# Router logits of a two-pass fp32 macaron block: rows moved past the split router instead of the router past the rows

## What is computed

```python
def route(x, router_w, bias):                    # x: rows x 128, router_w: 16 x 128
    logits = x @ router_w.T                      # one number per row and expert, in fp32
    s = sigmoid(logits) + bias
    # best 2 of 4 groups of experts, then the best 4 experts in them; weights normalised, times 2.5
    ...
h = silu(x @ gate_w[e]) * (x @ up_w[e])          # for each of 16 routed experts
y = sum_e weight[row, e] * (h @ down_w[e])       # plus 2 shared experts, unweighted
```

## Time and profile before

| | |
|---|---|
| median of three runs | 659.91 us |
| span of the profiled execution | 657.5 us |
| busy, PE (TensorE) | 648.0 us (99%) |
| busy, DVE (VectorE) | 550.5 us (84%) |
| busy, POOL (GpSimd) | 464.4 us (71%) |
| busy, ACT (ScalarE) | 400.7 us (61%) |
| granted TensorE clock | 1.000 in every stage |

### The profile page before, as it was taken

One profiled execution on the slowest core, in us unless ns is written; L12 is line 12 of the kernel. 1 busy time (PEld: TensorE's weight loads), 2 busy tenths in 40 slices (PEclk: granted clock), 3 DMA queues, 4 the chain that ended last, 5 costly groups with the idle time before them and its releaser, 6 DMA issues.

```text
span 657.5 us, 10122 instructions
## 1 busy us (share of the span) xinstructions
PE 648.0 (99%) x3043; PEld 534.3 (81%) x3043; DVE 550.5 (84%) x1468; ACT 400.7 (61%) x790; POOL 464.4 (71%) x400
## 2 busy tenths in 40 slices
PE   8999999999999999999999999999999999999997
PEld 7888888888788887888878888878878888888886
DVE  6899889797988979879798798896987979878674
ACT  5876666566675555755657556575564655655554
POOL 6997776767866678566785667766667677767664
PEclk9999999999999999999999999999999999999999
DMA  9827352816236152271532804526147172543510
GB/s 232 271 63 262 93 227 50 273 32 212 83 85 235 32 192 99 59 264 32 158 134 49 273 17 122 201 48 247 50 86 248 44 226 93 161 157 83 221 32 33
DMA packets 107542, 90.07 MB, mean 137 GB/s; under 512 B 67408, under 2 KB 89824, under 8 KB 107488
## 3 DMA queue, kind: packets, MB, share of 16 engines
q1 hardware_dynamic: 107488, 89.43, 43.1%
HBM read 79.45 MB, written 9.96 MB: 136 GB/s over the span
## 4 chain that ended last, share of the span: by engine, by line
PE 91%; DVE 7%; DMA 1%; issue 0%; SPq 0%; ACT 0%; DVEq 0%
PE gateP L512 10%; PE upP L512 9%; PE gateP L516 9%; PE gateP L513 9%; PE yP L516 9%; PE yP L512 9%; PE upP L516 9%; PE yP L513 9%; PE upP L513 9%; PE prepP L548 1%; DVE T L1226 1%; PE attP L565 1%; DVE ast L1153 1%; DVE A L1257 1%; DVE parts L961 1%; PE attP L617 1%
## 5 line engine op out<-in xcount | busy, mean ns | idle before, releaser
L396 POOL TENSOR_TENSOR A_lo<-A,A_hi 128x512 fp32r<-128x512 f32 x287 | 370.7, 1294 | 175.2 <-ACT A_hi L869 174.6
L895 ACT ACTIVATE gateP<-gateP 128x512 f32<-128x512 f32 x252 | 146.5, 581 | 161.9 <-PE gateP L516 161.1
L1226 DVE TENSOR_TENSOR T<-gateP,CB 128x512 f32<-128x512 f32 x252 | 172.8, 686 | 65.6 <-ACT gateP L895 63.3
L869 ACT CAST A_hi<-A 128x512 fp32r<-128x512 f32 x287 | 176.5, 615 | 51.0 <-DVE A L1257 48.8
L1257 DVE TENSOR_TENSOR A<-upP,T 128x512 f32<-128x512 f32 x254 | 175.7, 692 | 8.7
L512 PE MATMUL gateP<-XT_hi,W_hi 128*128 128x512 f32 x288 | 117.9, 409 | 2.9 <-DVE T L1226 2.8
L512 PE MATMUL yP<-A_hi,W_hi 128*128 128x512 f32 x288 | 113.0, 392 | 0.0
L516 PE MATMUL gateP<-XT_lo,W_hi 128*128 128x512 f32 x288 | 112.5, 391 | 0.0
L516 PE MATMUL yP<-A_lo,W_hi 128*128 128x512 f32 x288 | 112.4, 390 | 0.0
L513 PE MATMUL gateP<-XT_hi,W_lo 128*128 128x512 f32 x288 | 112.4, 390 | 0.0
L513 PE MATMUL yP<-A_hi,W_lo 128*128 128x512 f32 x288 | 112.1, 389 | 0.0
(11 more groups left out here) (229 smaller groups left out, 652.3 us busy)
## 6 DMA issues: line engine op xcount, KB each, us to landing
CB<-combT SPq DMA_DIRECT2D x126, 512.0 KB, 6.7
y_rows<-YB SPq DMA_DIRECT2D x60, 64.0 KB, 1.9
YP<-y_rows SPq DMA_DIRECT2D x15, 256.0 KB, 2.8
x_rows<-XN SPq DMA_DIRECT2D x13, 256.0 KB, 2.3
XB<-x_rows SPq DMA_DIRECT2D x52, 64.0 KB, 2.3
out_dram<-X SPq DMA_DIRECT2D x7, 256.0 KB, 5.3
X<-in_L_attn_x_dram SPq DMA_DIRECT2D x3, 512.0 KB, 9.5
W_in<-in_L_ffn_gate_w_dram SPq DMA_DIRECT2D x4, 256.0 KB, 5.2
```

The costliest lines, as they stand in the source:

```text
L396: pool.tensor_tensor(A_lo[:, slot, :], A[:, slot, :], A_hi[:, slot, :].bitcast(F32), ALU.subtract).then_inc(low_done, 1)
L869: act.copy(A_hi[:, v % SLOTS, :], A[:, v % SLOTS, :]).then_inc(high_done, 1)
L895: act.activation(dst, gateP[u % 2][:, :], ACT.Silu).then_inc(silu_done, 1)
L1226: dve.tensor_tensor(T[:, u % TS, :], silu, weights, ALU.mult).then_inc(gate_weighted, 1)
```

## The change

From the logits of step 2 on, the router is what is loaded as weights and the rows are what moves. Two new instructions, once per launch, split the router into a rounded part (ScalarE, at u = 6 of step 0) and a remainder (GpSimd, at u = 13 of step 0). They lie in `RT4`, four times side by side, so that its 128 columns are 4 copies x 16 experts x 2 parts. `XT_hi` and then `XT_lo` move past it, 512 columns each, and accumulate in the bank `backP`. There experts are on partitions and rows on columns. VectorE turns them back at the head of routing part 0: four transposes in squares of 32 x 32, one for each group of 32 partitions, from `backP` to `lgT`, and a reduction that adds the two parts of the router, from `lgT` to `prepP`, where TensorE wrote the logits before. Each of the two is followed by a wait for its end. The logits stand at u = 2 of a step (before: u = 1), behind the wait for `XT_lo`. `lgT` lies where `Wk_in` lay, which is used only in step 1's set-up, and `quad` shares its place with `Gn`.

```diff
@@ -143,6 +143,7 @@
         blkm = sb("blkm", [P, P])
         R_in = sb("R_in", [E, P])
         RT = sb("RT", [P, E])
+        RT4 = sb("RT4", [P, P // SQUARE, E, 2], F32R)
         ebias = sb("ebias", [P, E])
         Wq = sb("Wq", [P, P + 1])
         Wk_in = sb("Wk_in", [P, P])
@@ -177,7 +178,6 @@
         Mm = sb("Mm", [P, P])
         AT = sb("AT", [P, P + 1])
         Am = sb("Am", [P, P])
-        quad = sb("quad", [P, P])
         chvar = sb("chvar", [P, 1])
         chmean = sb("chmean", [P, 1])
         dev = sb("dev", [P, 1])
@@ -189,6 +189,8 @@
         zb = sb("zb", [P, P])
         ATs = sb("ATs", [P, P])
         Bm = P1
+        quad = Gn
+        lgT = Wk_in
         brow = Mf
 
 
@@ -456,6 +459,11 @@
                     early = first and s == 0
                     if early and u in SPLIT_AT:
                         split_low(SPLIT_AT[u])
+                    if first and u == 13:
+
+                        pool.wait_ge(router_split, 1)
+                        pool.tensor_tensor(RT4[:, :, :, 1], RT[:, :].unsqueeze(1).broadcast_to([P, P // SQUARE, E]),
+                                           RT4[:, :, :, 0].bitcast(F32), ALU.subtract).then_inc(router_split, 1)
                     if first and u == 24:
                         pool.memset(XA[:, :, :], 1.0)
                     if w == (14 if early else 3) and not last:
@@ -539,15 +547,30 @@
 
             def logits(t):
 
-                pe.wait_ge(xt_ready, t + 1)
-                bank = backP if isinstance(t, int) and t < 2 else prepP
-                if t >= 2:
-
-                    pe.wait_ge(route_seq, ROUTE_OPS * t)
-                for j in range(TILES):
-                    mm = pe.matmul(bank[:, j * E:(j + 1) * E], XT[:, j * P:(j + 1) * P], RT[:, :],
-                                   start=True, stop=True)
-                mm.then_inc(logits_done, 1)
+                if t < 2:
+                    pe.wait_ge(xt_ready, t + 1)
+                    for j in range(TILES):
+                        mm = pe.matmul(backP[:, j * E:(j + 1) * E], XT[:, j * P:(j + 1) * P], RT[:, :],
+                                       start=True, stop=True)
+                    mm.then_inc(logits_done, 1)
+                    return
+                if t == 2:
+
+                    pe.wait_ge(router_split, 2)
+                    pe.wait_ge(route_seq, ROUTE_OPS * (t - 1) + 2)
+                else:
+                    pe.wait_ge(logits_turned, t - 2)
+                b = (t - 1) // 2 - ATT0
+                if t % 2 and 0 < b <= BATCH:
+
+                    pe.wait_ge(attended, 2 * b + 2)
+                if t % 2 == 0 and 0 <= b < BATCH:
+
+                    pe.wait_ge(att_act, ATT_ACT * b + 5)
+                pe.wait_ge(xt_lo_ready, t + 1)
+                router = RT4[:, :, :, :].rearrange("p a e i -> p (a e i)")
+                pe.matmul(backP[:, :], router, XT_hi[:, t % 2, :], start=True, stop=False)
+                pe.matmul(backP[:, :], router, XT_lo[:, t % 2, :], start=False, stop=True).then_inc(logits_done, 1)
 
             def transpose_weights(t):
                 pe.wait_ge(route_seq, ROUTE_OPS * (t + 1))
@@ -571,6 +594,7 @@
                     if g == 0:
 
                         pe.wait_ge(attended, 2 * (b + 1))
+                        pe.wait_ge(logits_turned, 2 * (b + ATT0))
                     else:
 
                         pe.wait_ge(att_act, ATT_ACT * b + 2)
@@ -722,7 +746,7 @@
                         mm.then_inc(setup_psum, 1)
                     early = first and s == 0
                     if not (last and s >= 1):
-                        if w == (7 if early else 1):
+                        if w == (7 if early else 2):
                             logits(t0 + s + 1)
                     if early and w == 17:
                         transpose_next(2)
@@ -896,6 +920,11 @@
                     if first:
                         for unit in HIGH_AT.get(u, ()):
                             split_high(unit)
+                    if first and u == 6:
+
+                        act.wait_ge(setup_sb, 1)
+                        act.copy(RT4[:, :, :, 0], RT[:, :].unsqueeze(1).broadcast_to([P, P // SQUARE, E])
+                                 ).then_inc(router_split, 1)
                     if first and u == 20:
 
 
@@ -1038,7 +1067,20 @@
                 selp4 = selp.rearrange("p t (g i) -> p (t g) i", i=PER_GROUP)
                 if part == 0:
                     dve.wait_ge(logits_done, t + 1)
-                    flat = (backP if isinstance(t, int) and t < 2 else prepP)[:, 0:TILES * E]
+                    if t < 2:
+                        flat = backP[:, 0:TILES * E]
+                    else:
+
+                        for a in range(P // SQUARE):
+                            group = slice(a * SQUARE, (a + 1) * SQUARE)
+                            own = backP[group, :].rearrange("p (j a c) -> p a j c", j=TILES, c=SQUARE)[:, a]
+                            ins = dve.transpose(lgT[group, :].rearrange("p (j c) -> p j c", c=SQUARE), own)
+                        ins.then_inc(logits_turned, 1)
+                        flat = prepP[:, 0:TILES * E]
+                        dve.wait_ge(logits_turned, t - 1)
+                        dve.tensor_reduce(flat, lgT[:, :].rearrange("p (k i) -> p k i", i=2), AX.X,
+                                          ALU.add).then_inc(logits_summed, 1)
+                        dve.wait_ge(logits_summed, t - 1)
 
                     near_f = near[:, :, :].rearrange("p t e -> p (t e)")
 
```

More of the change, by code:

```diff
@@ L225, in macaron_kernel @@
         logits_done, silu_route, route_seq = sem("logits_done"), sem("silu_route"), sem("route_seq")
+        router_split, logits_turned, logits_summed = sem("router_split"), sem("logits_turned"), sem("logits_summed")
         norm_seq = sem("norm_seq")
```

## The result

| | before | after |
|---|---|---|
| median of the runs beside each other | 659.81 us (659.46 to 660.23, 6 runs) | 694.19 us (693.78 to 700.88, 6 runs) |
| ratio | | 1.0535, 95% interval 1.0508 to 1.0563 |
| span of the profiled execution | 657.5 us | 692.5 us |
| busy, PE / DVE / POOL / ACT | 648.0 / 550.5 / 464.4 / 400.7 us | 655.6 / 584.5 / 464.9 / 401.9 us |
| granted TensorE clock, mean | 1.000 | 0.995 (0.979 in the run of 700.88 us) |

The change costs 5.3%. The sign was right; the time lies 9 us above the upper end of the range. The span has grown by 35.0 us, where the working had 21.0.

What follows compares the result with a forecast made beforehand. VectorE was taken to bound the kernel by holding up TensorE; 1.69 us a step less spare time gave 21.0 us, span 657.5 to 678.5, plus 2.4 to the median: 680.9 us, 3.2% slower, range 672 to 685.

Steps and rivals of the forecast that it cites:

- the working: The prediction's calculation over steps 1 to 14: together 21.0 us added, the profiled span going from 657.5 to 678.5 us.
- VectorE binds: Attention steps 4 to 11: VectorE sets TensorE's time once a step, the gate pass starting 0.06 us after `T` ends.
- the turn: VectorE's added transposes, reduction and two waits at the head of routing part 0: 1.69 us a step, one after the other.
- Attention swallowed nothing: Rival, steps 4, 6, 8 and 10: ScalarE sets the point, four delays vanish, 6.8 us less, 674.1 us; chance 8%.
- the transposes did not overlap: Rival, routing part 0: the four transposes overlap, 1.35 us a step, sum 16.2 us, time 676.1 us; chance 25%.
- `XT_lo` made TensorE wait as said: Logits at u = 2, step 2: TensorE would arrive at 93.22 and wait for `XT_lo` until 93.76.
- the sum: Steps 1 to 14: each gets VectorE's 1.69 us less its spare time, together 21.0 us.
- spare time: How long before TensorE's up pass VectorE has finished `A`, less 0.17 us: none in steps 4 to 12, 0.32 in step 2.
- the 0.91 us of TensorE's logits: Old fp32 logits at u = 1, removed: 0.91 us a step, a gain judged not to be had here.
- gate weight loads waiting for `T` at 25 us: Sign expected in the changed profile: TensorE's gate weight loads wait for VectorE's `T` some 25 us instead of 6.3.
- The two passes: TensorE's new logits at u = 2: two passes of 512 columns, 0.46 us a step.
- Step 14's 0.5 us: Step 14, where VectorE takes no statistics and comes to u = 2 some 0.45 us earlier: 0.5 us longer.

## Why the prediction was wrong

**What was right.** VectorE binds, and the turn costs 1.64 us a step against 1.69, its four transposes one after the other (310 ns each against 302, 0.31 to 0.33 us from start to start). In step 4 `T` of u = 3 still ends 0.05 us before the gate pass of u = 5, in step 5 `T` of u = 7 0.05 us before that of u = 9:

```profile
236.77 0.68 DVE L1268 TENSOR_TENSOR T<-gateP,CB 128x512 f32<-128x512 f32 x1
```

```profile
237.50 0.50 PE L520 MATMUL gateP<-XT_hi,W_hi 128*128 128x512 f32 x1
```

By the Trainium skill, "VectorE: DVE Perf Modes", section "Two Vector instructions with no wait between them", the four had to be held against each other; the changed kernel's trace agrees: each starts 0.01 us after the end of the one ahead. Without `nmean` and the falls, the changed kernel's 35.0 us are 20.5; the working had 21.0. Attention swallowed nothing, the transposes did not overlap, and `XT_lo` made TensorE wait as said.

**The step that failed** is the sum: "Each step gets VectorE's 1.69 us less its spare time." It takes VectorE's other rows to last as long as before. They don't, because the work that was *removed*, the 0.91 us of TensorE's logits, was put down as worth nothing. It is worth nothing to TensorE, but it moved ScalarE's `A_hi` forward by 0.93 us (step 2, counted from the `A_lo` ahead of `XT_lo`), and GpSimd's `A_lo` behind it by 0.46, up to the end of `XT_lo` and so into the place where `nmean` runs: 1.04 us in 12 steps, 12.5 us. The prediction asked whether a faster TensorE would wait, and not whom else it would set going earlier. The trace of before had the evidence: two statistics rows of 4 elements that take 1.14 and 1.27 us, both ending with a GpSimd row, and `nmean` between two GpSimd rows in a gap of 0.42 us.

The Trainium skill has the rule, on the page "SBUF — State Buffer", section "SBUF: two separate sides": VectorE and GpSimd share a pair of SBUF ports as a lock, taken for a whole instruction by whoever starts first; VectorE needs it with two inputs from SBUF (against a GpSimd instruction that reads SBUF), or in a mode that reads one input through two ports. The trace agrees: 1.15 and 1.25 us with two inputs, 1.21 for `nmean` with one, 0.17 when `nmean` starts ahead, 0.15 with its input in PSUM. That `nmean` runs in such a mode is read from its durations alone.

**The second** is a term that the sum doesn't have, TensorE's clock. The sum makes TensorE wait longer and lets it work on at the old pace. In steps 6 and 10 it did not: behind idle stretches of 1.84 and 0.71 us the clock fell to 1.2 GHz for 3.4 us. That is 2.0 us in the profiled execution, more in the run of 700.88 us. The length of the stretches alone doesn't decide: the same ones left the clock at 1.000 in steps 4 and 8, and with the old logits kept 0.85 and 0.71 us went ahead of a fall in each of steps 4, 6, 8 and 10. What decides stays open.

**Wrong without effect** was the wait that should have shown it: gate weight loads waiting for `T` at 25 us. They show 9.1, since the delay met the down product of u = 4 first; with ScalarE's silu moved behind the copy it is 29.2. The two passes take 0.54 us behind the wait for `XT_lo`, not 0.46; VectorE comes later still. Step 14's 0.5 us came out, though not by its working alone: with `XT_lo` earlier that step is 0.17 us shorter than before, so TensorE's wait for `XT_lo` had a part in it.

## What to carry to other kernels

When work is removed from an engine that isn't the bound, follow the earlier start through every engine behind it and ask what it will now run beside. Tiny VectorE rows that take over a microsecond and end with a GpSimd row aren't VectorE's work: count how many a step has, and look for the ones that escape through a gap. A stall can have a price beyond its length, where TensorE's clock falls behind it, and which wait it is booked under says little about who causes it.

## What the runs showed of the hardware

- A VectorE instruction of 128 x 4 elements in SBUF takes 0.15 to 0.17 us, or up to 1.3 us beside GpSimd's subtraction of 128 x 512, until that ends: 0.01 us ahead of its start is enough to escape. From PSUM, `nmean` takes 0.15 us beside the same.
- TensorE's clock fell from 2.4 to 1.2 GHz for 3.4 us behind idle stretches of 1.84 and 0.71 us, and in another kernel of 0.85 and 0.71 us, at about 1.0 us a fall; elsewhere it stayed up behind the same stretches, and executions of one kernel differ in how often it falls (the changed kernel with the old logits kept: a span of 677.7 us at a mean clock of 1.000, 682.3 at 0.990). Repeating products whose result is thrown away held it up.
- Eight passes of 128 columns take 0.85 us where two of 512 take 0.47.
